# Where two passes' parts are added: in DRAM as they are made, or in SBUF as they are loaded

## The reference, cut to what matters

```python
W = weights[condition]                        # one 64 x 64 matrix for each of the 32 batches
c = einsum('bct,bcd->bdt', x, W)              # x is (32, 64, 1024)
h = gelu(einsum('bsd,df->bsf', c, inter_w) + inter_b)     # 1024 -> 4096
out = x + einsum('bsf,fd->bsd', h, output_w) + output_b   # 4096 -> 1024
```

## Time and profile before

| | us |
|---|---|
| median of three runs (1225.93 to 1226.38) | 1226.2 |
| the profiled execution | 1227.55 |
| its span, first to last instruction | 1225.7 |

### The profile page before, as it was taken

The page is one execution under the profiler, slowest core; times in us unless marked ns, Lnnn a source line. Parts: engine busy times, 40 slices in busy tenths (PEclk is TensorE's granted clock), DMA queues, the critical chain, the costliest instruction groups (busy, mean ns, idle before and its releaser), DMA issues.

```text
span 1225.7 us, 15191 instructions
## 1 busy us (share of the span) xinstructions
PE 1212.6 (99%) x5468; PEld 1008.9 (82%) x5468; DVE 886.6 (72%) x1132; ACT 561.9 (46%) x961; POOL 274.3 (22%) x188
## 2 busy tenths in 40 slices
PE   9999999999999999999999799999999999999999
PEld 9888888888878888888888688888888888888887
DVE  5988788777548656666557478677788676787886
ACT  4755555555444444444444244444444444444443
POOL 3362233212306233432302220101110101101000
PEclk9999999999999999999999899999999999999999
DMA  9587667866996644666399995756863749956653
GB/s 346 161 294 260 220 235 279 302 245 223 402 389 198 156 135 100 185 181 169 79 362 279 329 284 189 237 174 170 195 170 117 191 120 247 289 184 187 189 146 112
DMA packets 119868, 267.62 MB, mean 218 GB/s; under 512 B 9938, under 2 KB 19442, under 8 KB 118386
## 3 DMA queue, kind: packets, MB, share of 16 engines
q1 hardware_dynamic: 105248, 232.81, 53.9%
q0 software_dynamic: 13824, 33.56, 16.0%
q10 hardware_dynamic: 722, 0.28, 0.1%
HBM read 174.34 MB, written 92.27 MB: 218 GB/s over the span
## 4 chain that ended last, share of the span: by engine, by line
PE 96%; DMA 2%; issue 1%; DVE 1%; POOL 0%; ACT 0%; SPq 0%; DVEq 0%; ACTq 0%
PE ps L691 49%; PE ps L707 44%; PE ps L639 1%; PE ps L654 1%; DMA p_mem<-c 1%; DMA out<-in_L_ffn_output_b_dram 1%; PE ps L726 0%; PE ps L734 0%; DVE part L983 0%; POOL out L607 0%; DVE rhs L1063 0%; DVE lhs L1060 0%; POOL p_mem L555 0%; ACT c L799 0%; DVE part L979 0%
## 5 line engine op out<-in xcount | busy, mean ns | idle before, releaser
L691 PE MATMUL ps<-y,lhs 128*128 128x512 f32 x2688 | 611.2, 389 | 2.0 <-ACT c L795 1.4
L691 PEld LDWEIGHTS ps<-y,lhs 128*128 128x128 f32 x2688 | 504.0, 188 | 107.0 <-ACT c L795 1.8
L707 PE MATMUL ps<-rhs,lhs 128*128 128x512 f32 x2472 | 563.1, 390 | 7.2 <-DVE rhs L1063 7.2
L707 PEld LDWEIGHTS ps<-rhs,lhs 128*128 128x128 f32 x2472 | 465.6, 188 | 104.5 <-DVE lhs L1060 7.6
L877 ACT ACTIVATE lhs<-h_raw 128x512 fp32r<-128x512 f32 x208 | 131.8, 634 | 332.6 <-PE ps L707 324.9
L1060 DVE TENSOR_TENSOR lhs<-h_raw,lhs 128x512 fp32r<-128x512 f32 x208 | 144.1, 693 | 123.8 <-ACT lhs L877 123.7
L964 DVE TENSOR_TENSOR lhs<-w_raw,lhs 128x512 fp32r<-128x512 f32 x128 | 114.6, 897 | 125.9 <-ACT lhs L790 125.9
L790 ACT ACTIVATE lhs<-w_raw 128x512 fp32r<-128x512 f32 x128 | 81.1, 634 | 171.5 <-PE ps L691 169.0
L1063 DVE TENSOR_TENSOR rhs<-w_buf,rhs 128x512 fp32r<-128x512 f32 x208 | 142.3, 684 | 0.0
L882 ACT ACTIVATE rhs<-w_buf 128x512 fp32r<-128x512 f32 x208 | 128.1, 616 | 0.0
L964 DVE TENSOR_TENSOR lhs<-s_w,lhs 128x512 fp32r<-128x512 f32 x96 | 74.2, 777 | 60.5 <-ACT lhs L790 60.3
(11 more groups left out here) (51 smaller groups left out, 553.0 us busy)
## 6 DMA issues: line engine op xcount, KB each, us to landing
h_raw<-p_mem SPq DMA_DIRECT2D x80, 512.0 KB, 4.9
w_raw<-in_L_ffn_inter_w_dram SPq DMA_DIRECT2D x31, 1024.0 KB, 7.9
p_mem<-part SPq DMA_DIRECT2D x96, 256.0 KB, 6.3
w_buf<-in_L_ffn_output_w_dram SPq DMA_DIRECT2D x12, 2048.0 KB, 14.6
q_mem<-part SPq DMA_DIRECT2D x64, 256.0 KB, 6.4
h_raw<-q_mem POOLq DMA_DIRECT2D x32, 512.0 KB, 7.7
y_mem<-y_out SPq DMA_DIRECT2D x28, 512.0 KB, 3.5
y<-y_mem SPq DMA_DIRECT2D x7, 2048.0 KB, 13.4
```

What stands on the lines that cost most here:

```text
L691: last = nc.tensor.matmul(ps[:, bank, :], w[:, k, :], y[i][:, part, k, :], start=(i in FRESH and k == 0 and u == 0), stop=(k == KH - 1 and ...
L707: last = nc.tensor.matmul(ps[:, bank2(t, tb), :], lhs[s % RING][:, a, blk(tb)], rhs[r][:, w, :], start=(t in FRESH2 and q == 0 and u == 0) ...
```

## The change

The four products that were summed in DRAM are now summed as they are loaded, as the other eight. The slots 15 and 16 of `p_mem` go; `q_mem` gets the slots 10 (`part[8]`) and 11 (`part[7]`), stored by SyncE as all others, the second of them at the new step `c == 6`. `sum_0`, `sum_2` and their semaphores go. GpSimd's list begins its second stage with `add_b2` for two blocks only; the others stand between the `add_second`s, of which there are now 48 and not 32: pairs 8 to 19 and 24 to 27 are new.

```diff
-P_PART = (0, 1, 15, 16, 4, None, 3, ...)
-Q_PART = (None, None, None, None, None, 0, None, ...)
-P_PARTS, Q_PARTS = 17, 10
-SUM_0 = (15, 16, 4)
-SUM_2 = (3,)
+P_PART = (0, 1, 2, 3, 4, None, 3, ...)
+Q_PART = (None, None, 10, 10, 10, 0, 11, ...)
+P_PARTS, Q_PARTS = 15, 12
...
-                    keep_part(p_mem, 16, n, 8)
...
-                    keep_part(p_mem, 15, n, 4)
...
                 if c == 1:
+                    keep_part(q_mem, 10, n, 8)
                     keep_part(q_mem, 3, n, 0)
...
+                if c == 6:
+                    keep_part(q_mem, 11, n, 7)
...
                 if n == 6:
                     keep_second(GROUPS - 1, 5)
+                    keep_second(GROUPS - 1, 6)
...
-                if n >= NG + 2:
-                    sum_0(n - 2)
...
-                if n >= NG + 2:
-                    sum_2(n - 2)
-            for n in range(GROUPS - 2, GROUPS):
-                sum_0(n)
-                sum_2(n)
...
-            for b in ("10", "01", "30", "00", "31", "21", "20"):
-                add_b2(b)
+            add_b2("10")
+            add_b2("01")
             for k in range(NPART):
-                wait_kept(pool, k, GROUPS)
+                pool.wait_ge(part_kept[k], 16 * GROUPS)
             pool.wait_ge(g11_kept, 16 * NG)
             for n in range(PAIRS):
+                if n == 10:
+                    add_b2("30")
+                if n == 14:
+                    add_b2("00")
+                if n == 20:
+                    add_b2("31")
+                if n == 28:
+                    add_b2("21")
+                    add_b2("20")
                 if n == 60:
                     add_b2("11")
                 if summed(n):
                     add_second(n)
```

More of the change, by code:

```diff
@@ L35 @@
 FRESH2 = (0, 1, 6, 7, 8, 10, 17, 18, 19, 20, 21, 25)
-P_PART = (0, 1, 15, 16, 4, None, 3, None, 5, None, 6, 7, None, None, 8, 6, 9, 10, 11, 12, None, 2, 13, 12, 14, 13)
-Q_PART = (None, None, None, None, None, 0, None, 1, None, 2, 3, 4, 3, 5, None, 6, None, 3, 7, 8, 7, None, 7, None, None, 9)
-P_PARTS, Q_PARTS = 17, 10
-SUM_0 = (15, 16, 4)
-SUM_2 = (3,)
+P_PART = (0, 1, 2, 3, 4, None, 3, None, 5, None, 6, 7, None, None, 8, 6, 9, 10, 11, 12, None, 2, 13, 12, 14, 13)
+Q_PART = (None, None, 10, 10, 10, 0, 11, 1, None, 2, 3, 4, 3, 5, None, 6, None, 3, 7, 8, 7, None, 7, None, None, 9)
+P_PARTS, Q_PARTS = 15, 12
 BUFFER = (0, 1, 0, 0, 3, 0, 2, 0, 1, 2, 0, 6, 5, 2, 1, 4, 3, 0, 2, 5, 0, 3, 0, 2, 1, 0)
@@ L152, in build @@
         part_kept = [sem(f"part_kept{i}") for i in range(NPART)]
-        summed_0, summed_2 = sem("summed_0"), sem("summed_2")
         out_done, out_ended = sem("out_done"), sem("out_ended")
@@ L236, in sums @@
             return sum(summed(i) for i in range(n % HRING, n + 1, HRING))
[L238 to L250, removed]
         def y1_item(n, c):
@@ L431, in _ @@
                             sp.wait_ge(lhs_lo, step1(n - 1, CHUNKS))
-                            wait_kept(sp, 0, NG)
+                            sp.wait_ge(part_kept[0], 16 * NG)
                             for i in range(HRING - 1):
@@ L446, in _ @@
                     sp.wait_ge(c11_kept, 32 * NG)
-                    wait_kept(sp, 8, GROUPS)
-                    wait_kept(sp, 9, GROUPS)
+                    sp.wait_ge(part_kept[8], 16 * GROUPS)
+                    sp.wait_ge(part_kept[9], 16 * GROUPS)
                 if n == 5:
@@ L457, in _ @@
                     for k in (1, 2, 3, 4, 5, 6, 7):
-                        wait_kept(sp, k, NG)
+                        sp.wait_ge(part_kept[k], 16 * NG)
                     for done in (c12_kept, c21_kept, c22_kept):
@@ L478, in _ @@
                     for k in range(NPART):
-                        wait_kept(sp, k, GROUPS)
+                        sp.wait_ge(part_kept[k], 16 * GROUPS)
                     sp.wait_ge(g11_kept, 16 * NG)
@@ L551, in picks1 @@
                 pool.wait_ge(picked1, end_j * PER)
[L553 to L569, removed]
             picks1(0, TILES)
@@ L817, in negate @@
                 act.wait_ge(of_made, 2 * n + 2 if k == 8 or n >= NG else 2 * n + 1)
-                wait_kept(act, k, n)
+                if n > 0:
+                    act.wait_ge(part_kept[k], 16 * n)
                 nc.scalar.activation(part[k][:], of, ACT.Copy, scale=-1.0).then_inc(part_made[k], 1)
@@ L977, in begin @@
             def begin(k, n, a, b, op):
-                wait_kept(dve, k, n)
+                if n > 0:
+                    dve.wait_ge(part_kept[k], 16 * n)
                 nc.vector.tensor_tensor(part[k][:], a, b, op).then_inc(part_begun, 1)
             def combine(k, n, a, b, op):
-                wait_kept(dve, k, n)
+                if n > 0:
+                    dve.wait_ge(part_kept[k], 16 * n)
                 nc.vector.tensor_tensor(part[k][:], a, b, op).then_inc(part_made[k], 1)
```

## The result

| | before | changed | ratio (95% interval) |
|---|---|---|---|
| median, us | 1226.07 (4 runs) | 1240.85 (4 runs, 1239.84 to 1243.5) | 1.0123 (1.0108 to 1.0138) |
| profiled execution | 1227.55 | 1241.49 | |
| its span | 1225.7 | 1239.7 | |

Slower by 14.8 us. The sign is as forecast; the size, +6.3, is less than half of it, and the median lies 0.85 us above the upper end of the forecast's own range (1228.7 to 1240).

A forecast was written before the change was run, and what follows sets the result against it. TensorE was taken as the bound, busy 1212.6 of 1225.7 us. Gain -9.6, pair 10 +10.6, slow clock +2.4, pair 14 +3.2 sum to +6.6 on 1226.2: 1232.8, stated as 1232.5; own range 1228.7 to 1240.

The forecast's parts named there:

- gain of 9.6 us: TensorE's hole ahead of 684.44, blamed on block 10's late bias, goes: 7.2 us plus 2.4 of slow clock.
- (2): GpSimd's queue up to pair 10: add 10 lands at 714.6, TensorE 14.0 us late; lower end 7.2.
- the middle: Lateness at pair 10 taken as 10.6 us, between 14.0 and 7.2, the latter with bias DMAs without pauses.
- Step (1): Start of the adds: pair 8's load lands 4.4 us earlier, at 684; ends 680 and 688.5.
- Step (3): TensorE's clock falls again after the hole at pair 10: 2.4 us.
- step (4): From add 10 to add 14 the queue makes TensorE late by a further 5.4 or 1.0 us, middle 3.2.
- What goes: DRAM sums and two 256 KB writes per group go; no other TensorE hole found hangs on them; SyncE only moves forward.
- The forecast's mechanism: Load-time adds and bias DMAs in GpSimd's queue come late for TensorE at pairs 10 and 14; chance 0.48.
- Rival A: The adds keep up, add 10 landing before 700.6; only the removed stall counts: 1216.6, up to 1223; chance 0.24.
- Rival C: Shared DMA engines give out (share 1.07), late loads make a third hole, ended by `h_raw<-p_mem` or weights: 1241 to 1246; chance 0.10.
- would never lag: By the skill's rule, 3.2 us per 512 KB add and 2.6 per bias DMA, GpSimd's queue keeps up.

The follow-up runs named there:

- Experiments 4: Kernel before with block 10's bias added ahead of the last DRAM sum, all sums still in DRAM: 1227.45 us, ratio 1.0005.
- 12: Kernel before with twice the room for GpSimd's DMA descriptors and nothing else: 1228.04 us, ratio 1.0011.
- experiment 3: Changed kernel with block 30's 2 MB of weights loaded ahead of pair 10's load instead of pair 6's: 1239.56 us, ratio 1.0101 to before.
- experiment 1: Changed kernel with the bias additions of blocks 30 and 00 left out: 1225.09 us, ratio 0.9983 to before.
- experiment 7: Changed kernel with the bias of five blocks added by GpSimd itself from one SBUF copy, not by accumulating DMAs: 1228.7 us, ratio 1.001 to before.
- Experiment 11: Changed kernel with plain copies in place of the accumulating DMAs of pairs 8 to 19: 1231.98 us, ratio 1.004 to before.
- experiment 5: Changed kernel with block 31's 2 MB weights load on SyncE cut to 64 KB: 1239.55 us, ratio 1.009 to before.
- 6: Changed kernel with bias blocks 30 and 00 two pairs later in GpSimd's list, ahead of pairs 12 and 16: 1239.65 us, ratio 1.0088 to before.
- experiment 10: Changed kernel with five blocks' bias added by GpSimd, block 30's weights ahead of pair 10's load, twice the descriptor room: 1226.57 us, ratio 0.9999 to before.
- experiment 2: Changed kernel with twice the room for GpSimd's DMA descriptors, 2048 instead of 1024 bytes a partition: 1237.2 us, ratio 1.0082 to before.
- experiments 8: Kernel before with five blocks' bias added by GpSimd itself and block 10's bias DMAs ahead of the last DRAM sum: 1226.18 us, ratio 0.9987.
- 9: Kernel before with five blocks' bias by GpSimd, block 10's bias earlier, block 30's weights ahead of pair 10's load, twice the descriptor room: 1218.76 us, ratio 0.9939.

## Why the prediction was right in sign and too small in size

**The gain of 9.6 us held in the sum, but not on the one wait that it was read from.** The old hole is gone in the changed kernel, so this term isn't what failed. But the step "Gain: 9.6 us" took the hole as the price of block 10's bias and left all other DMAs as they were. Experiments 4 (by order) and 12 (by room) brought bias DMAs forward and changed nothing else, and pair 6's load, in time at 678.3 before, landed at 684.9 and 686.4 and made a hole of the same size. In the changed kernel it landed at 678.0, as before, but TensorE was 2.1 us further ahead: 2.3 us of hole and 1.8 of slow clock ahead of and behind 680.21. The prediction gave a due time for pair 4's load and none for those of pairs 5 to 7.

**The step that failed is (2): its route to pair 10 was right, and the middle taken from it was the mistake.** Step (1) put pair 8's load at 684: the add went out at 685.00. Step (2)'s upper end had add 10 landed at 714.6: it landed at 706.71 + 8.0 = 714.7. The queue behaved as its rows had said, pauses and all. I then took the middle between that end and one without pauses, which no row of a full queue with bias DMAs showed. TensorE was 17.2 us late at pair 10 (holes and slow clock of pairs 6 and 8 included: 2.3 + 1.8 + 2.7 + 1.6 + 8.7), where I took 10.6: of the 6.6, 3.4 are the middle, 2.1 the earlier begin of the second stage, which makes each pair due earlier, and about 1 the rest. Pair 10 had to wait for add 10 in any case, so the two holes and the slow clock ahead of it are part of the 17.2 and cost nothing beside it; experiment 3, which removed both, was only 1.3 us faster.

**The slow clock was charged once.** Step (3) gave 2.4 us; behind pair 10 it was 2.9. But the lateness was split over four holes, each with its own. Those at pairs 6 and 8 are in the 17.2; the one behind pair 14, 1.8, I left out. Pair 14's own hole was 3.8, for 3.2 in step (4).

**"What goes" was costed at nothing and was worth 2.1 us.** The second stage began earlier with the DRAM sums gone: TensorE's first step of it at 645.1 to 646.5 in the traces of the nine kernels with twelve products added at the load, and at 646.0 to 647.5 in the seven with DRAM sums. By the medians of the two groups it is 1.5. The 1.36 us hole at 352 of the kernel before is part of it: all seven with DRAM sums have a hole there (0.7 to 1.4 us), none of the nine has.

So, in the terms of the sum: 6.6 forecast, + 6.6 at pair 10, + 0.5 and + 1.8 of slow clock, + 0.6 at pair 14, - 2.1: 14.0, the measured difference of the spans.

**Theories.** The forecast's mechanism, that GpSimd's DMAs can't be served in time, holds: 1, 7 and 11, which take work out of GpSimd's queue, gave 15.8, 12.2 and 8.9 us; 3, 5 and 6, which ease SyncE's queue or reorder, 1.2 to 1.3; the room, 3.6. Rival A (the adds keep up) is out. Rival C (the shared engines give out) was right about the share, 1.04, and its sign, a hole ended by `h_raw<-p_mem`, did come, but at pair 6, ahead of all adds; SyncE's 2 MB less hardly helped. How much of the queue's slowness is its own and how much its share of the engines is open: in all these runs both queues were busy together.

The Trainium skill (DMA: Bandwidth & Descriptors, section Anatomy of one DMA) would have had a 512 KB DMA in 3.2 us by its fit, for which the prediction gave A a chance. Taken one after the other, the prediction's estimates from that fit give 3.2 + 3.2 + 4 x 2.6 + 3.2 = 20.0 us and add 10 at 704.7, still 4 us after the 700.6 that rival A needs: that the queue "would never lag" by it was too strong. Experiment 11 bears on it: the copies were 1.2 us of 16 engines cheaper than the accumulates, so a rate for copies is too good for adds. In the full queue the two copies issued around 705 landed 9.8 us after their issue in the median, most of it behind the DMAs ahead of them, since they landed 1.2 us apart.

## What to carry to other kernels

Before counting a hole as gain, take the wait that ends it away on paper and ask when each other input of the next steps is there, and by how much it is in time. An input that is only just in time (0.3 us here) can be made late by the very DMAs that are brought forward. Here two moves that did nothing alone gave 8 us together. When work moves from a stretch with spare DMA time to one that is full, price it by the queue's rate when full, and where rows show that rate, pauses included, don't take a middle with a kinder one. Split lateness can cost more than its sum: each of the changed kernel's four holes brought its own stretch of slow clock, though not every hole of the experiments did. When work moves from DMAs to GpSimd, look for single VectorE instructions that grow beside it, and not only at VectorE's sum: three of some 6 us made all the large holes of experiment 10.

## What the runs showed of the hardware that I had not expected

The pauses between GpSimd's DMAs are the room for their descriptors: with 1024 bytes at most three went out together and the fourth of a bias block only when the queue was empty; with 2048 bytes four and more followed at once.

The length of a hole doesn't tell what the clock does behind it. In the changed kernel holes of 2.3 and 8.7 us both brought the level of 1.2 GHz, worth 1.8 and 2.9 us. But behind 3.16 us in experiment 1 and 2.77 in experiment 5 the granted clock stayed at 1.00, while 1.82 us in experiment 7 brought a mean of 0.58 over the next 3.5 us. Nor does the loss grow with the hole: it was 3.0 us behind 2.94 in experiment 2 (first row) and 2.0 behind 9.68 in experiment 3 (second row), by 2.73 us for 12 matmuls:

```profile
681.12 13.93 PE L675 MATMUL ps<-rhs,lhs 128*128 128x512 f32 x48 [2.94 <-DVE rhs L1034]
```

```profile
709.76 23.79 PE L676 MATMUL ps<-rhs,lhs 128*128 128x512 f32 x96 [9.68 <-DVE rhs L1035]
```

An accumulating DMA of 512 KB took 1.2 us more of all 16 engines than a copy of the same bytes.

A VectorE split of 0.69 us took 5.4 to 6.1 us, six times in experiments 7 and 10, each time beside four GpSimd additions of 128x512 in a row and until the last of them had ended. In experiments 8 and 9 the same additions only stretched each VectorE instruction to at most 2.3 us. What decides between the two no run shows.
